# Two of the four output streams of each token tile move from VectorE to Pool in the mixing part of a decoder layer

## What is computed

```python
def _L2_ffn_ref(x, W_res, W_pre, W_post, ...):      # x is the layer norm of the residual
    ...
    H_res = sinkhorn_log(H_res_logits)              # [B, T, 4, 4], 50 iterations
    H_pre = jax.nn.softmax(H_pre_logits, axis=-1)   # [B, T, 4]
    H_post = jax.nn.softmax(H_post_logits, axis=-1)
    g = jax.nn.sigmoid(gate)[0]
    H_res = (1.0 - g) * I + g * H_res
    x_streams = x.reshape(B, T, n, C)               # n = 4 streams, C = 128
    x_pre = jnp.einsum('btnc,btn->btc', x_streams, H_pre)
    y = x_pre @ W_branch
    x_mixed = jnp.einsum('btij,btjc->btic', H_res, x_streams)
    y_distributed = jnp.einsum('btc,btn->btnc', y, H_post)
    return (x_mixed + y_distributed).reshape(B, T, nC)
# the caller: x = x + _L2_ffn_ref(_layernorm(x), ...)
```

## Time and profile before

| | before |
|---|---|
| median of 3 runs | 4574.91 us (4573.71 to 4575.09) |
| the profiled execution, its own time | 4574.2 us |
| span of that execution | 4572.4 us |
| busy share of the span: TensorE, VectorE, ScalarE, Pool | 88%, 47%, 32%, 6% |
| mixing block | from 2881.5 us to about 2959 us of the span |

### The profile page before, as it was taken

How to read it: one execution, slowest core, us unless ns; L and a number is a source line. 1 busy time by engine, 2 the same in 40 slices (tenths; PEclk the granted TensorE clock), 3 DMA queues, 4 the chain that set the end, 5 groups by cost and what they waited for, 6 DMA issues and landing times. The chain is left out here.

```text
span 4572.4 us, 53045 instructions
## 1 busy us (share of the span) xinstructions
PE 4042.3 (88%) x19210; PEld 2182.7 (48%) x19210; DVE 2145.2 (47%) x3722; ACT 1440.6 (32%) x2619; POOL 291.7 (6%) x223
## 2 busy tenths in 40 slices
PE   7899979997696999988988669699999789999996
PEld 3334335553373545543436554355555355556553
DVE  0777755552163322223338418766556244344532
ACT  3777735551142211111113234212112132223321
POOL 1011011110001000000000011000000000000001
PEclk9999989998797999998988879899999899999998
DMA  4111211101002322210000021200000021111100
GB/s 170 53 56 49 67 66 36 35 33 40 13 11 107 120 97 98 83 48 32 0 25 1 38 93 33 68 31 19 18 37 19 0 62 33 33 37 61 33 5 21
DMA packets 130444, 214.88 MB, mean 47 GB/s; under 512 B 42576, under 2 KB 92880, under 8 KB 119360
## 3 DMA queue, kind: packets, MB, share of 16 engines
q1 hardware_dynamic: 130240, 212.06, 13.5%
HBM read 167.99 MB, written 44.04 MB: 46 GB/s over the span
## 5 line engine op out<-in xcount | busy, mean ns | idle before, releaser
L341 PE MATMUL l1x_pj<-kvT,l1x_wq 128*128 128x512 f32 x512 | 234.1, 611 | 8.7 <-DMA l1x_wq<-in_L_xattn_Wq 8.7
L705 PE MATMUL l3x_pj<-kvT,l3x_wq 128*128 128x512 f32 x512 | 232.4, 608 | 3.5 <-issue 3.5
L803 PE MATMUL l3a_po<-l3a_wo,l3a_cT 128*128 128x512 f32 x512 | 230.6, 604 | 3.4 <-ACT l3a_cT L930 3.2
L386 PE MATMUL l1x_po<-l1x_wo,l1x_cT 128*128 128x512 f32 x512 | 226.3, 596 | 1.2 <-issue 1.2
L705 PE MATMUL l3a_pj<-kvT,l3a_wq 128*128 128x512 f32 x512 | 224.9, 592 | 0.0
L479 DVE TENSOR_TENSOR x<-x,l1x_po 128x512 f32<-128x512 f32 x64 | 44.1, 689 | 278.6 <-PE l1x_po L386 278.6
L341 PEld LDWEIGHTS l1x_pj<-kvT,l1x_wq 128*128 128x128 f32 x512 | 96.9, 194 | 122.1 <-issue 110.7
L705 PEld LDWEIGHTS l3x_pj<-kvT,l3x_wq 128*128 128x128 f32 x512 | 98.0, 195 | 119.3 <-issue 119.3
L803 PEld LDWEIGHTS l3a_po<-l3a_wo,l3a_cT 128*128 128x128 f32 x512 | 95.6, 192 | 121.6 <-issue 112.6
L386 PEld LDWEIGHTS l1x_po<-l1x_wo,l1x_cT 128*128 128x128 f32 x512 | 95.7, 192 | 111.0 <-issue 111.0
L705 PEld LDWEIGHTS l3a_pj<-kvT,l3a_wq 128*128 128x128 f32 x512 | 95.4, 190 | 111.6 <-issue 111.0
(11 more groups left out here) (568 smaller groups left out, 7772.6 us busy)
## 6 DMA issues: line engine op xcount, KB each, us to landing
l1x_kb<-l1x_keys SPq DMA_DIRECT2D x32, 512.0 KB, 4.7
l1x_vb<-l1x_values SPq DMA_DIRECT2D x32, 512.0 KB, 3.4
l1x_keys<-l0a_kv SPq DMA_DIRECT2D x48, 256.0 KB, 2.0
l1x_values<-l0a_kv SPq DMA_DIRECT2D x40, 256.0 KB, 2.3
kvT<-in_L_xattn_Wv SPq DMA_DIRECT2D x8, 1024.0 KB, 5.6
l1x_wq<-in_L_xattn_Wq SPq DMA_DIRECT2D x8, 1024.0 KB, 4.8
l1x_sbias<-in_L_xattn_bias SPq DMA_DIRECT2D x8, 1024.0 KB, 6.8
l1x_wo<-in_L_xattn_Wo SPq DMA_DIRECT2D x8, 1024.0 KB, 6.9
```

The lines of the kernel that those rows point to most:

```text
L341: mm = pe.matmul(pj[:, j, :], wq[:, u, k, h * DH:(h + 1) * DH], m.kvT[:, k, 1, 512 * j:512 * (j + 1)], start=k == 0, stop=k == KC - 1)
L386: mm = pe.matmul(po[:, t % 2, :], cT[:, u, h, t * P:(t + 1) * P], wo[:, u, h, :], start=h == 0, stop=h == GH - 1)
L705: mm = pe.matmul(pj[:, j, :], wq[:, u, k, h * DH:(h + 1) * DH], m.kvT[:, k, 1, 512 * j:512 * (j + 1)], start=k == 0, stop=k == KC - 1)
L803: mm = pe.matmul(outs[t % 2][:, :], cT[:, h, t * P:(t + 1) * P], wo[:, u, h, :], start=h == 0, stop=h == GH - 1)
```

## The change

Two of the four output streams (i = 2 and 3) of every tile are formed on Pool, streams 0 and 1 stay on VectorE. Pool does the work without the fused multiply-and-add of VectorE: for one output stream i it has four instructions, each of which waits for the one before (`pool_mixed`): the product of all four input streams with the weights of i into a new buffer `share` (128x512, the second operand a broadcast of `tm[n, i, :]`), the sum of its upper and lower half (128x256), and two additions of 128x128 into the residual. VectorE's loop over i runs to 2 in place of 4, so it has eight mixing instructions per tile, and its final additions, which still cover all four streams, wait for `pool_mixed` besides `y`. ScalarE's write of `xs` waits from the third tile on for Pool to be done with the tile that used the slot. Pool's work for tile n + 1 stands ahead of the `rstd` of tile n.

```diff
+POOLED = 2
...
+                def mix(n):
+                    xs_j = xs[:, n % 2, :].rearrange("p (j c) -> p j c", c=CW)
+                    pool.wait_ge(xs_ready, n + 2)
+                    for k in range(POOLED):
+                        i = NS - POOLED + k
+                        own = m.x[:, n, i * CW:(i + 1) * CW]
+                        behind = 4 * (POOLED * n + k) + 1
+                        pool.wait_ge(pool_mixed, behind)
+                        nc.gpsimd.tensor_tensor(share[:, :, :], xs_j, tm[:, n, i, :].unsqueeze(2).to_broadcast([P, NS, CW]),
+                                                ALU.mult).then_inc(pool_mixed, 1)
+                        pool.wait_ge(pool_mixed, behind + 1)
+                        nc.gpsimd.tensor_tensor(share[:, 0:2, :], share[:, 0:2, :], share[:, 2:4, :], ALU.add).then_inc(pool_mixed, 1)
+                        pool.wait_ge(pool_mixed, behind + 2)
+                        nc.gpsimd.tensor_tensor(own, own, share[:, 0, :], ALU.add).then_inc(pool_mixed, 1)
+                        pool.wait_ge(pool_mixed, behind + 3)
+                        nc.gpsimd.tensor_tensor(own, own, share[:, 1, :], ALU.add).then_inc(pool_mixed, 1)
+
+                mix(0)
                 for n in range(T):
+                    if n + 1 < T:
+                        mix(n + 1)
                     pool.wait_ge(n_half, n + 2)
...
                     act.wait_ge(mixed, n if u else n + 1)
+                    if n >= 2:
+                        act.wait_ge(pool_mixed, 4 * POOLED * (n - 1) + 1)
...
-                        for i in range(NS):
+                        for i in range(NS - POOLED):
                             nc.vector.scalar_tensor_tensor(res(i), stream(j), tm[:, n, i, j:j + 1], res(i),
...
                     dve.wait_ge(mix_link, chain.behind)
+                    dve.wait_ge(pool_mixed, 4 * POOLED * (n + 1) + 1)
```

More of the change, by code:

```diff
@@ L2500, in stage_l2_ffn @@
         preT_ready, y_ready, mixed = st.sem("preT_ready"), st.sem("y_ready"), st.sem("mixed")
-        mix_link = st.sem("mix_link")
+        mix_link, pool_mixed = st.sem("mix_link"), st.sem("pool_mixed")
+        share = st.sb("share", [P, NS, CW])
         UNITS3 = FOLD + CTX_K + CTX_V
@@ L2912, in body @@
                 def body(n, u):
-                    per = 3 + NS * (NS - 1) + NS
+                    per = 3 + NS * (NS - POOLED)
                     chain.at(per * n)
```

## The result

| | before | after |
|---|---|---|
| median of 6 runs each | 4574.22 us (4570.06 to 4575.09) | 4599.22 us (4598.20 to 4602.52) |
| ratio, 95% interval | | 1.0057 (1.0044 to 1.0070) |
| span of the profiled execution | 4572.4 us | 4597.0 us |
| first VectorE instruction of the block | 2882.35 | 2884.50 |
| from there to the start of the last tile's final additions | 71.9 us | 89.9 us |

The sign was as forecast, the size was not: 25.0 us in the medians, 24.6 in the spans. Of the 24.6, 2.15 had been lost before the block began, in code that the change does not touch, 18.4 lie between the block's first instruction and the next stage's first product, and 4.1 behind that.

A forecast was written before the change was run, and what follows sets the result against it. TensorE's chain pre, unit, `y` bounds tiles with slow units, VectorE the others. 4 x 1.28 + 3 x 1.37 + 1.28 = 10.5, plus 0.5 for the clock, gives +11.0 us: 4585.9 us, range 4577 to 4593.

The forecast's parts named there:

- nothing is held: Rival for VectorE beside Pool: this operation does not compete with Pool; 4572.5 us, not slower, chance 0.12.
- the first instruction of `pre`: Start of a tile's VectorE chain: first `pre` instruction ends unheld; later ones meet Pool, so TensorE gets `pre` 1.28 us later.
- the row of the reductions: Sinkhorn-loop reductions on VectorE with one SBUF operand, never above 383 ns, read as not held by Pool.
- the alternation: VectorE's mixing beside Pool: each engine waits for the other; mixing ends at 7.39 instead of 6.02, 1.37 us later.
- the walk: One tile followed instruction by instruction: `pre` 1.28 us later, mixing ending at 7.39 and Pool at 6.27.
- its own formula: Block's delay: four intervals into odd tiles at 1.28, three into even tiles at 1.37, last tile 1.28; together 10.5 us.
- the sum of 11.0: Whole predicted loss: 10.5 us of tile delays plus 0.5 us for slower TensorE units.
- the clock's term: TensorE's units at the lower granted clock: at most 1.2 us if all ran slow, 0.5 taken.
- the prediction's own base of 4574.9: Median time of the kernel before, to which the predicted 11.0 us was added; the profiled execution lay 0.7 below it.
- unsplit pairs: Rival for mixing: VectorE's two mixing instructions pass before Pool is served, Pool ends last; +8.3, 4583 us, chance 0.20.
- the rival in which each engine is held for the other's whole instruction: VectorE and Pool handovers each cost 0.09 to 0.14 more; mixing ends at 9.3; +19.4, 4594 us, chance 0.10.

The follow-up runs named there:

- The small fillings: Four extra TensorE matmul instructions per tile behind `y`, in the kernel with pre and mixing in PSUM (two streams on Pool) and the kernel before: 4574.43 and 4574.59 us.
- the one with the repeated instruction: The kernel before, Pool unchanged, with the first instruction of `pre` carried out six times: 4604.25 against 4576.04 us, ratio 1.0059.

## Why the prediction was right in kind and wrong in size

**Right: what decides.** Neither VectorE's count of instructions nor Pool's throughput sets the end of a tile, but when `pre` reaches TensorE and what follows from it, and Pool's work beside VectorE delays it. It delays the end of mixing too, but in the change itself that decided nothing: the final additions waited for `y` in all eight tiles. The rival "nothing is held" is out by the trace, and by the run in which Pool worked on scratch data. Pool's durations were 1.04, 0.73, 0.46 and 0.46 with gaps of 0.08, as taken from the earlier trace rows.

**Wrong: the first instruction of `pre`.** The prediction let it pass unhindered, as an instruction with one operand from SBUF, by the reductions of the earlier trace rows, and reckoned 1.28 us for the rest. It was held in all eight tiles, 0.88 us each (1165 ns against 286), and then the second met Pool's 256-wide addition: TensorE got `pre` 1.66 us later. To let it pass was wrong for this operation; the row of the reductions does not carry over to it. With its result in PSUM it took 0.35 us and was not held. The Trainium skill says this: page "SBUF — State Buffer", section "Who interferes with whom", lists tensor_scalar among the operations that can take both read ports, and page "VectorE: DVE Perf Modes", section "What auto-detection actually checks", requires source and result in SBUF for that. The trace agrees twice over: held from SBUF to SBUF, and longer by 68 ns (354 against 286) but not held when it writes PSUM. The prediction used the first of these sections only for the operations with two inputs.

**Wrong in mechanism, right in number by luck: the alternation.** Mixing was to end at 7.39 and ended at 7.39. But the walk had both engines wait for each other in turn, with Pool ending at 6.27. In fact Pool was never held in this kernel (its products all lie within 1040 to 1043 ns) and ended at 5.95, and VectorE took all of the waiting. The first tile shows VectorE's record 0.05 us ahead of Pool's and VectorE held all the same. The Trainium skill, page "SBUF — State Buffer", section "Who interferes with whom", says that issue order decides who is blocked; by the order of the records alone the trace does not bear that out. In the run on scratch data VectorE's first record was 0.10 us ahead, and there it went through in 0.28 us and Pool's product took 1.08.

**Wrong, and the larger part of the miss in the block: TensorE's clock.** The prediction saw that a unit takes 3.61 or 5.30 us, took 5.30 as the slow case, and gave the extra slow units 0.5 us, 1.2 at most. By its own formula, with the measured 1.66 in place of 1.28, the block would have grown by 4 x 1.66 + 3 x 1.37 + 1.66 = 12.4 us. It grew by 18.0, so what was left to the term taken at 0.5 was 5.6. The formula's path was wrong as well: it had three intervals follow mixing, and all seven followed `y`. Two things were missed. 5.30 is not the end: units took up to 6.48. And the clock feeds back: a later `pre` makes `y` later and the tile longer, TensorE stands still for longer in each tile, more of the block runs at 1.2 GHz, and the slower units make `y` later again. The granted clock of the block, 0.88 before and 0.77 after, means by the two levels that about 24% and 46% of it ran at 1.2 GHz (an estimate). TensorE's idle time ahead of the transposition stands in brackets at the end of a row; two tiles in a row of the kernel before, which none of the groups ahead has:

```profile
2892.19 0.33 PE L2882 MATMUL l2f_pt<-ident,l2f_pre 128*128 128x128 f32 x1 [2.65 <-DVE l2f_pre L2933]
2901.16 0.33 PE L2882 MATMUL l2f_pt<-ident,l2f_pre 128*128 128x128 f32 x1 [4.97 <-DVE l2f_pre L2933]
```

The unit behind the first of these took 3.61 us, behind the second 5.30. The same two tiles after the change:

```profile
2898.75 0.48 PE L2909 MATMUL l2f_pt<-ident,l2f_pre 128*128 128x128 f32 x1 [4.30 <-DVE l2f_pre L2960]
2910.33 0.43 PE L2909 MATMUL l2f_pt<-ident,l2f_pre 128*128 128x128 f32 x1 [5.21 <-DVE l2f_pre L2960]
```

The units behind them took 5.88 and 5.24. Before, a short wait (2.65 to 3.11) and a long one took turns for most of the block; after, the shortest is 4.30, and no unit stays at 3.6. But the wait ahead of a unit does not settle how that unit runs. The transposition of tile 5 in the kernel before, and its unit:

```profile
2927.77 0.33 PE L2882 MATMUL l2f_pt<-ident,l2f_pre 128*128 128x128 f32 x1 [2.87 <-DVE l2f_pre L2933]
2927.94 5.30 PE L2526 MATMUL l2f_pf<-l2f_w_v,kvT 128*128 128x512 f32 x8
```

The small fillings cut the waits by some 1.7 us and left the units nearly as they were. The two halves of the loop are shown by a run each: with no Pool work a delay of 1.6 us per tile brought the clock to 0.79 and the block to +17.0, where the delay alone would give 8 x 1.61 = 12.9; and ten filling instructions raised the clock to 0.96 and took 10.2 us off the block, part of it through Pool's head start in three tiles.

**Outside the block: 6.6 us that no term covered.** In spans the sum of 11.0 fell short by 13.6 us: 1.9 by `pre`, 5.1 by the clock's term, and 6.6 outside the block. With the block's 18.0 alone the prediction's own base of 4574.9 gives 4592.9, the upper end of its range of 4577 to 4593. Of the 6.6, 2.15 lie ahead of the block, in instructions that are the same, and 0.4 between its end and the next stage; single executions of the kernel before range from 4570.04 to 4588.37 us in one of these comparisons, so 2.15 may be chance. The 4.1 behind are three pieces: 1.1 in the first products of the next stage, which take 9.9 us in place of 8.8; 1.1 in that attention stage (604.7 us for its query products in place of 603.6); and 1.8 at a jump on a flag near the end, where VectorE stands for 5.48 us instead of 3.71:

```profile
4508.67 4.85 DVE L127 BATCH_NORM_STATS2 l3f_stats<-x 128x6 f32<-128x512 f32 x8 [3.71 <-PEq L89]
```

```profile
4532.61 4.85 DVE L127 BATCH_NORM_STATS2 l3f_stats<-x 128x6 f32<-128x512 f32 x8 [5.48 <-PEq L89]
```

The first row is of before, the second of after. From the same instruction of the norm before it (`l3m_stats`) to this row it is 15.0 or 15.1 us in the change and in all eight kernels made from it, whatever their block took, and 13.3 in the kernel before and in three of the four made from that one (15.3 in the one with the repeated instruction). So these 1.8 us go with the changed program but not with how long its mixing takes; what in the program makes them was not tried and stays open.

**The rivals.** Pool ended well before VectorE, so unsplit pairs is out. The time, 4599, lay even above the rival in which each engine is held for the other's whole instruction (4594), but not for its reason: VectorE's mixing ended at 7.39, not 9.3. What made the time was the clock's term, which the sum had at 1.2 at most, and what lay outside the block. The range, 4577 to 4593, took its width from the uncertain holds and next to none from the clock.

## What to carry over

When work moves to Pool, look at which VectorE instructions run beside it: here those that read two tensors from SBUF, and tensor_scalar from SBUF to SBUF, were held by Pool's work, and what waits for them may be worth more than what was moved. Partial sums in PSUM took the hold away for 0.08 us per tile (`pre` at 1.58 instead of 1.50 us, with Pool busy beside it). And where TensorE stands idle between short pieces, price a delay of its input by rows in which its clock is at either level, and leave width for it in the range: a delay of 1.6 us per tile with no Pool work cost 2.1 us per tile here (17.0 over eight). Putting `y` ahead of the long unit gave the fastest kernel, with `pre` in time; whether it also takes the price off a late `pre` was not tried.

## What was not expected of the hardware

- After the change Pool's chain of instructions always got through and VectorE took the waits: over 16 products Pool's spread was 3 ns, while VectorE's mixing instructions ranged from 343 to 1197 ns. The earlier trace rows had shown Pool held by a VectorE instruction of 1.22 us; here none was that long by itself. In other kernels Pool was held now and then, by little: 1078 in place of 1041 ns for the first product on scratch data, and up to 0.61 in place of 0.455 us for an addition of 128 in kernels with `pre` in PSUM.
- A tensor_scalar of 128x128 in float32 with a per-partition factor takes 286 ns from SBUF to SBUF and was held there up to 1166; to PSUM it took 341 to 355 and was held in no tile of the five kernels that write it there.
- A scalar_tensor_tensor costs the same with its running sum in PSUM as in SBUF (0.74 for two in a chain).
- The unit of eight matmuls took anything from 3.60 to 6.48 us. With ten filling instructions per tile behind `y` it stayed at 3.6 from tile 1 on; four, in two other kernels, changed one unit of fourteen by more than 0.1 us.
